# Four PSUM banks for the maxima's scores and one for the output, another order of blocks, and GpSimd for the parts of the turned maxima

## The chip, the cores and the metric

The program runs on one core of a Trainium2 chip. The metric is the device time of one execution in microseconds (us). The engines are TensorE (PE in the profile, its weight loads PEld), VectorE (DVE), ScalarE (ACT), GpSimd (POOL) and the queue from which DMAs are issued (SP). PSUM has eight banks of 128 x 512 fp32 elements; PE writes its products there.

## The reference, cut to what matters

One transformer layer on 4 sequences of 1024 tokens, 256 wide: a routed feed-forward part (8 experts, each token takes 2), an attention with 16 heads of 16, and the same feed-forward part again.

```python
x = x + 0.5 * ffn(layernorm(x))
x = x + attn(layernorm(x))        # adds its own residual and a second layernorm inside
x = x + 0.5 * ffn(layernorm(x))
# inside attn, for each of the 4 x 16 heads:
scores = (q @ k.T) * 0.25         # 1024 x 1024, causal
attn = softmax(scores)            # exp(score - row maximum) / row sum
out = attn @ v
```

Only the attention is touched by the change, and four lines of the transition into it.

## The kernel before, in words

The program has three parts in time: the first feed-forward part with the q, k and v projections, the attention, and the output projection with the second feed-forward part. The attention works on 16 groups (`NG`) of 4 heads of one sequence. Each engine runs its own list of instructions per group (`slot(g)`), in an order written out by hand, and waits on semaphores.

A group's work on PE is of three kinds.

- **Scores for the maxima** (`max_scores`, line 1404, 48 matmuls a group): queries x keys, in 38 units of 512 PSUM columns, each in a bank of `ms`. VectorE takes the negative row maximum of each unit (`max_read`; line 1431 for units with the causal diagonal, one instruction a head; line 1435 for whole ones). This runs one to two groups ahead. When all maxima of group g+1 stand, PE turns them (line 1397, the 39th entry), VectorE copies the turned tile out of PSUM (line 1413) and splits it with a cast, a subtraction, a cast and a subtraction (lines 1417 to 1423) into three bf16 parts, and SP places the parts by three DMAs as three more rows of the queries (`place_maxima`, line 1464; semaphore `mplaced`).
- **Scores for the exponentials** (`exp_unit`, line 1565, 48 matmuls a group): keys x queries with the maxima's rows, so that the maximum is already subtracted. The 12 blocks of a group (4 of the first half of the queries, 8 of the second) make 38 units in three banks `es`. The first unit of a group waits for `mplaced`. ScalarE takes the exponential of each unit into one of four buffers `probs` (line 1544). For blocks 0 to 3 and 8 to 11 GpSimd then zeroes what lies beyond the diagonal (line 1515).
- **Products** (`products`, line 1581): a block's probabilities by the values, fp32, 4 heads side by side in 32 columns of the array each; 8 records a block. They add up in a bank of `os`, one bank for each half of the queries. ScalarE copies each bank out when its half is complete (`copy_out`, line 1531, behind blocks 1 and 5 of its own order).

How these follow each other on PE is given by three tables with an entry a block: `MAXIMA` (how many entries of the maxima's stream go among that block's exponential units; `FIRST_MAXIMA` for group 0, `LAST_MAXIMA` for the last two groups), `MAXIMUM_FIRST` (whether such an entry comes first), and `PRODUCTS` (after which step, and for how many blocks, products are made; they run behind by at least two blocks). Blocks of products made at one place, or at the end of one block's steps and the start of the next, follow each other without scores between them. With the tables of before a group has products at nine places, three of them with two blocks.

Three banks serve the maxima's scores (`ms`), so PE may be two units ahead of VectorE:

```python
a.ms = ms = s.banks[3:6]
a.os = os_ = s.banks[6:8]
...
pe.wait_ge(mread, at(position - 2))
```

GpSimd's list for a group is the eight selects, and a copy of the next group's values behind block 2. SP's list for a group is: 12 loads of queries and keys for group g+2, 8 stores of group g-1, the three DMAs of `place_maxima(g+1)`, and 4 stores of inverted sums.

Of the kernel before, what the change touches and what calls it, by code (L numbers as in the profile page):

```python
# [18 lines left out]
ALU = mybir.AluOpType  # L19
ACT = mybir.ActivationFunctionType  # L20
# [32 lines left out]

FIRST = (39, 42, 47, 50)


CREDIT = 8

# [2 lines left out]

MAXIMA = (3, 3, 2, 3, 5, 4, 4, 3, 4, 3, 4, 1)
FIRST_MAXIMA = (6, 3, 2, 3, 5, 4, 4, 3, 4, 3, 4, 1)
LAST_MAXIMA = (3, 3, 2, 2, 3, 3, 3, 3, 2, 1, 0, 0)
MAXIMUM_FIRST = (1, 1, 1, 1, 0, 0, 1, 1, 1, 0, 0, 1)
BEHIND = -2
PRODUCTS = ((0, 0), (1, 2), (3, 1), (6, 1), (8, 2), (8, 1), (0, 0), (7, 2), (8, 1), (0, 0), (2, 1), (0, 1))


def at(events):
# [96 lines left out]
def ffn(nc, s, ctx, a, first):  # L169
# [96 lines left out]


    if first:
        ring, pb, pt, pr = [a.ms[2], a.es[2], *a.os], a.ms[1], a.es[0:2], a.ms[0]
    else:  # L270
        ring, pb, pt, pr = [*a.es, a.os[0]], a.os[1], a.ms[0:2], a.ms[2]
    pr_b = pr[:, 0:P // 2].bitcast(BF16)
    if first:

# [474 lines left out]
    def tensor(pe):  # L749
# [180 lines left out]
            pe.wait_ge(a.o_copied, at(2 * NG))  # L930
        slots(pe, slot)
        if first:
            pe.wait_ge(q.qk_rest, at(4 * (NCH - 1) + 1))
            a.first_scores(pe, FIRST[2], FIRST[3])
            pe.wait_ge(q.v_ready, at(2 * NCH))
            pe.wait_ge(q.qk_rest, at(4 * NCH))
# [303 lines left out]
def attention(nc, s, ctx):  # L1240
# [11 lines left out]
    early = 14  # L1252
    nkb = len(keys)
    half_blocks = CH // P
    assert nmax % 3 == 0
    offset = s.behind_v

    def sb(name, shape, dt=F32):
# [32 lines left out]
    below = sb("below", [P, CH], BF16)  # L1291
    masked_b = below[:, CH - P:CH]
    a.es = es = s.banks[0:3]
    a.ms = ms = s.banks[3:6]
    a.os = os_ = s.banks[6:8]

    consts, vones = sem("consts"), sem("vones")
    loaded = [sem(f"loaded{u}") for u in range(3)]
# [30 lines left out]

    def place(g, n):  # L1330

        return nmax + early + nmax * g.n + n, (early + n) % 3

    def placed(g):

# [55 lines left out]

    def max_scores(pe, entry, position, bank):
        g, n = entry
        pe.wait_ge(mread, at(position - 2))
        if n is None:
            pe.wait_ge(mfinal, at(g.n + 1))
            nc.tensor.transpose(ms[bank][0:GH * KT, 0:P], neg1[g.u][:].rearrange("p c i -> p (c i)"),  # L1397
                                s.ident[:]).then_inc(mscore, 1)
            return
        if n == 0:  # L1400
            pe.wait_ge(loaded[g.u], at(16 * 12 * (g.turn + 1)))
        i, lo, width, heads, diagonal = munits[n]
        for a, c in enumerate(heads):
            last = nc.tensor.matmul(ms[bank][:, a * width:(a + 1) * width], qs[g.u][0:ROWS, c, i * P:(i + 1) * P],  # L1404
                                    ks[g.u][0:ROWS, c, lo:lo + width], start=True, stop=True)
        last.then_inc(mscore, 1)

    def max_read(dve, entry, position, bank):
        g, n = entry
        dve.wait_ge(mscore, at(position + 1))  # L1410
        if n is None:
            t, r, m = turned, turned_rest, mparts[g.u]
            dve.tensor_copy(t[:], ms[bank][0:GH * KT, 0:P]).then_inc(mread, 1)
            dve.wait_ge(mread, at(position + 1))
            if not (isinstance(g.turn, int) and g.turn == 0):
                dve.wait_ge(mplaced[g.u], at(16 * 3 * g.turn))
            dve.tensor_copy(m[:, 0, :], t[:]).then_inc(mpart, 1)
            dve.wait_ge(mpart, at(5 * g.n + 1))
            dve.tensor_tensor(r[:], t[:], m[:, 0, :], ALU.subtract).then_inc(mpart, 1)
            dve.wait_ge(mpart, at(5 * g.n + 2))  # L1420
            dve.tensor_copy(m[:, 1, :], r[:]).then_inc(mpart, 1)
            dve.wait_ge(mpart, at(5 * g.n + 3))
            dve.tensor_tensor(m[:, 2, :], r[:], m[:, 1, :], ALU.subtract).then_inc(mpart, 2)
            return
        i, lo, width, heads, diagonal = munits[n]
        dst = neg1[g.u][:, heads[0]:heads[0] + len(heads), i:i + 1] if lo == 0 else \
            neg2[g.u][:, heads[0]:heads[0] + len(heads), i - CH // P:i - CH // P + 1]
        if diagonal:
            for a in range(len(heads)):
                part = ms[bank][:, a * width:(a + 1) * width]  # L1430
                last = dve.tensor_tensor_reduce(part, part, below[:, CH - width:CH], -1.0, 3.0e38, ALU.add, ALU.min,  # L1431
                                                dst[:, a, :])
            last.then_inc(mread, 1)
        else:
            dve.tensor_reduce(dst, ms[bank][:, 0:len(heads) * width].rearrange("p (h w) -> p h w", w=width), AX.X,  # L1435
                              ALU.max, negate=True).then_inc(mread, 1)
        if n == len(munits) - 1:
            dve.wait_ge(mread, at(position + 1))
            late = neg1[g.u][:, :, CH // P:KT]
            dve.tensor_tensor(late, late, neg2[g.u][:], ALU.min).then_inc(mfinal, 1)  # L1440

    def first_bank(position):

        if position < FIRST[0]:
            return 0
        return (position - FIRST[0]) % 2 if position < FIRST[2] else position % 3

    def first_scores(pe, lo, hi):

# [57 lines left out]
    def gpsimd(pool, lead):  # L1507
        def slot(g):
            for b, (j, half, start, width) in enumerate(keys):
                if b in sel_blocks:  # L1510
                    pool.wait_ge(expd, at(nexp * g.n + unit0[b + 1]))
                    pool.sem_inc(apart, 1)
                    part = probs[b % 4][:, :, 0:P]

                    pool.affine_select(out=part, in_=part, compare_op=ALU.is_ge, fill=0.0, base=0,  # L1515
                                       pattern=[[0, GH], [1, P]], channel_multiplier=-1).then_inc(kept, 1)
                if b == 2 and exists(g + 1):
                    pool.wait_ge(summed, at(nkb * g.n))
                    copy_values(pool, g + 1)
                lead_step(lead, g, b)  # L1520

        slots(slot)

    def scalar(act, lead):
        def copy_out(g, half):
            act.wait_ge(summed, at(nkb * g.n + (4 if half == 0 else nkb)))
            if exists(g + (-2)):
                old = g + (-2)
                act.wait_ge(stored[old.u], at(16 * GH * (old.turn + 1)))
                act.wait_ge(den_placed[old.u], at(16 * GH * (old.turn + 1)))  # L1530
            act.activation(oev[g.n % 2][:, half * CH:(half + 1) * CH], os_[half][:], ACT.Copy).then_inc(o_copied, 1)

        def slot(g):
            for b, (j, half, start, width) in enumerate(keys):
# [21 lines left out]
    def tensor(pe, lead):  # L1556
# [13 lines left out]
        def products(g, b):  # L1570
# [5 lines left out]
            if b == 0:  # L1576
                pe.wait_ge(v_copied, at(g.n + 1))
            if j == 0:
                pe.wait_ge(o_copied, at(2 * g.n - 1 + half))
            for c in range(GH):  # L1580
                last = nc.tensor.matmul(os_[half][SLOT * c:SLOT * (c + 1), start:CH], vs[g.n % 2][:, j, c, :],  # L1581
                                        probs[b % 4][:, c, 0:width], start=(j == 0),
                                        stop=(j == (half + 1) * CH // P - 1))
            last.then_inc(summed, 1)
# [81 lines left out]
```

## Time and the profile before

| | before |
|---|---|
| median of 3 runs | 1008.99 us (1007.57 to 1012.28) |
| the profiled execution, its own time | 1006.76 us |
| its span in the profile | 1005.0 us |
| the three parts in the span | about 0 to 335, 335 to 745, 745 to 1005 us |
| PE busy in the attention, 335 to 745 | 403.94 of 410 us |
| VectorE busy there | 388.97 us |
| ScalarE busy there | 305.94 us |
| GpSimd busy there | 96.83 us |

The profile is of one execution. Its own time lies 1.8 us above its span, and 2.2 us below the median of the runs. Busy time of PE is modelled, with matmuls overlapping, so it is read by the starts of the matmuls and not by their length. A semaphore's release is inferred.

### The profile page before, as it was taken

Reading aid. Unit: us, or ns where it says so; the run is one execution under the profiler, and the core shown is the slowest. Engines: PE = TensorE matmul, PEld = TensorE weight load, DVE = VectorE, ACT = ScalarE, POOL = GpSimd, SP = SyncE. Lnnn points to the kernel's source line nnn. Section 1 sums busy time; section 2 is a strip of 40 time slices with the busy share of each in tenths; the row PEclk is TensorE's granted clock in tenths of the full one; section 3 lists DMA queues with packets and bytes.
Section 4 is the critical chain, followed back from the end, with each engine's and each line's share of the span. In section 5 each row is a group of like instructions: output and inputs, shape, how many; then the busy total and the mean of one; then the engine's idle time right before and its main releaser. Section 6 shows DMA issues by size and latency. Waiting matters only on the chain.

```text
span 1005.0 us, 17657 instructions
## 1 busy us (share of the span) xinstructions
PE 956.5 (95%) x5602; PEld 569.3 (57%) x5602; DVE 831.5 (83%) x2445; ACT 511.8 (51%) x1053; POOL 264.9 (26%) x288
## 2 busy tenths in 40 slices
PE   6899998988998899999999999999998999999998
PEld 4678886766766433333333333333343777777776
DVE  6677777777677799999999999999868888888775
ACT  4235434414133577777777777777765333232310
POOL 1012204202021622121212212121443543435211
PEclk9999999999999999999999999999999999999999
DMA  6301121101032422222222223223320111110001
GB/s 214 98 1 64 57 70 64 58 6 63 1 95 65 139 77 66 67 71 68 70 67 71 77 77 77 76 76 77 69 84 12 44 64 64 63 49 16 19 22 42
DMA packets 55109, 64.32 MB, mean 64 GB/s; under 512 B 13824, under 2 KB 37360, under 8 KB 55024
## 3 DMA queue, kind: packets, MB, share of 16 engines
q1 hardware_dynamic: 54432, 62.47, 21.9%
q8 instruction: 43, 0.70, 0.3%
q10 hardware_dynamic: 592, 0.80, 0.2%
q14 instruction: 42, 0.34, 0.1%
HBM read 41.30 MB, written 21.23 MB: 62 GB/s over the span
## 4 chain that ended last, share of the span: by engine, by line
PE 65%; DVE 5%; ACT 2%; POOL 1%; issue 1%; DVEq 0%; ACTq 0%; POOLq 0%
PE bank L362 21%; PE bank L1581 14%; PE bank L1404 13%; PE bank L1565 13%; PE bank L836 2%; ACT b_probs L1544 1%; PE bank L354 1%; POOL b_ks L1377 1%; POOL a_part L496 1%; DVE c_acc L1049 1%; DVE c_st L317 1%; DVE bank L1431 0%; PE bank L785 0%; DVE c_eq L1010 0%; PE bank L1397 0%
## 5 line engine op out<-in xcount | busy, mean ns | idle before, releaser
L1544 ACT ACTIVATE b_probs<-bank 128x512 f32<-128x512 f32 (+1 forms) x608 | 302.4, 585 | 110.4 <-PE bank L1565 110.1
L1431 DVE CUSTOM_DVE_ANT_0 bank<-bank,b_below 128x384 f32<-128x384 f32 (+3 forms) x512 | 235.4, 516 | 11.1 <-PE bank L1404 9.7
L1404 PE MATMUL bank<-b_ks,b_qs 96*128 96x512 bf16 (+3 forms) x768 | 222.0, 330 | 16.4 <-DVE b_neg L1431 8.8
L1565 PE MATMUL bank<-b_qs,b_ks 99*128 99x512 bf16 (+3 forms) x768 | 214.5, 330 | 4.5 <-ACT b_probs L1544 4.3
L362 PE MATMUL bank<-we,a_xt 128*128 128x512 f32 x768 | 194.5, 405 | 0.9 <-DVE a_acc L1049 0.9
L362 PE MATMUL bank<-we,c_xt 128*128 128x512 f32 x768 | 186.2, 398 | 1.1 <-DVE c_acc L1049 0.9
L1515 POOL TENSOR_SCALAR_AFFINE_SELECT b_probs<-b_probs 128x512 f32<-128x512 f32 x128 | 84.3, 659 | 323.1 <-ACT b_probs L1544 320.0
L1435 DVE TENSOR_REDUCE b_neg<-bank 128x1 f32<-128x512 f32 x256 | 161.1, 680 | 2.6 <-PE bank L1404 1.2
L362 PEld LDWEIGHTS bank<-we,c_xt 128*128 128x128 f32 x768 | 142.3, 188 | 33.6 <-DVE c_acc L1049 2.0
L362 PEld LDWEIGHTS bank<-we,a_xt 128*128 128x128 f32 x768 | 142.7, 191 | 28.7 <-DVE a_acc L1049 1.4
L1581 PE MATMUL bank<-b_probs,b_vs 128*32 128x512 f32 (+3 forms) x1536 | 155.7, 500 | 1.2 <-POOL b_probs L1515 1.2
L1404 PEld LDWEIGHTS bank<-b_ks,b_qs 96*128 96x128 bf16 x768 | 67.3, 97 | 123.7 <-DVE b_neg L1431 54.9
L1565 PEld LDWEIGHTS bank<-b_qs,b_ks 99*128 99x128 bf16 x768 | 66.1, 98 | 107.8 <-ACT b_probs L1544 70.1
L1049 DVE SCALAR_TENSOR_TENSOR a_acc<-bank,a_mask,a_acc 128x256 f32<-128x256 f32 x192 | 81.7, 477 | 19.5 <-PE bank L362 18.8
L1049 DVE SCALAR_TENSOR_TENSOR c_acc<-bank,c_mask,c_acc 128x256 f32<-128x256 f32 x190 | 80.1, 477 | 19.8 <-PE bank L362 19.2
L490 POOL TENSOR_TENSOR xs<-a_acc,a_acc 128x256 f32<-128x256 f32 x32 | 25.2, 788 | 237.3 <-DVE a_acc L1049 237.3
L1431 DVE DVE_READ_ACCUMULATOR2_ANT b_neg<- 128x1 f32 x512 | 70.4, 137 | 0.0
L1581 PEld LDWEIGHTS bank<-b_probs,b_vs 128*32 128x32 f32 x1536 | 35.3, 109 | 57.1 <-ACT b_probs L1544 34.7
L490 POOL TENSOR_TENSOR xs<-c_acc,c_acc 128x256 f32 (+1 forms) x31 | 28.4, 916 | 94.1 <-DVE c_acc L1049 94.1
L362 PE MATMUL bank<-a_xt2r,a_wqk 128*128 128x512 f32 x192 | 46.4, 396 | 0.0
L333 ACT ACTIVATE c_std<-c_mv,eps 128x4 f32<-128x4 f32 x16 | 4.9, 303 | 80.4 <-DVE c_mv L322 80.4
L333 ACT ACTIVATE a_std<-a_mv,eps 128x4 f32<-128x4 f32 x16 | 4.8, 298 | 75.5 <-DVE a_mv L322 75.5
(136 smaller groups left out, 925.7 us busy)
## 6 DMA issues: line engine op xcount, KB each, us to landing
b_qs<-q_parts SPq DMA_DIRECT2D x96, 128.0 KB, 3.0
b_ks<-k_parts SPq DMA_DIRECT2D x96, 128.0 KB, 3.0
q_parts<-a_part SPq DMA_DIRECT2D x16, 384.0 KB, 2.6
k_parts<-a_part SPq DMA_DIRECT2D x16, 384.0 KB, 2.7
att_num<-b_oev SPq DMA_DIRECT2D x64, 64.0 KB, 2.2
c_num<-att_num SPq DMA_DIRECT2D x8, 512.0 KB
c_rec<-att_rec SPq DMA_DIRECT2D x16, 256.0 KB
out<-xs SPq DMA_DIRECT2D x7, 512.0 KB, 3.2
```

The lines of the kernel that those rows point to most:

```text
L317: last = dve.bn_stats(st_[:, t, :], src(t))
L362: last = nc.tensor.matmul(out_, wa if x_moves else xa_, xa_ if x_moves else wa, start=(n == 0), stop=(n == len(steps) - 1))
L490: pool.tensor_tensor(s.xs[:, row(c, t), :].rearrange("p a d -> p (a d)"), acc[t % 2][0][:], acc[t % 2][1][:], ALU.add).then_inc(q.x_ready, 1)
L836: last = nc.tensor.matmul(pt[pair][:, i * D:(i + 1) * D], att[par][:, h, t * P:(t + 1) * P], s.wp[:, h, :], start=(h == 0), stop=(h == DK ...
L1049: dve.scalar_tensor_tensor(out=dst[:], in0=ring[n][:, i * D:(i + 1) * D], scalar=mask[par][:, t, 2 * n + i:2 * n + i + 1], in1=base, op0=A ...
L1404: last = nc.tensor.matmul(ms[bank][:, a * width:(a + 1) * width], qs[g.u][0:ROWS, c, i * P:(i + 1) * P], ks[g.u][0:ROWS, c, lo:lo + width] ...
L1431: last = dve.tensor_tensor_reduce(part, part, below[:, CH - width:CH], -1.0, 3.0e38, ALU.add, ALU.min, dst[:, a, :])
L1435: dve.tensor_reduce(dst, ms[bank][:, 0:len(heads) * width].rearrange("p (h w) -> p h w", w=width), AX.X, ALU.max, negate=True).then_inc(mr ...
L1515: pool.affine_select(out=part, in_=part, compare_op=ALU.is_ge, fill=0.0, base=0, pattern=[[0, GH], [1, P]], channel_multiplier=-1).then_in ...
L1544: act.activation(probs[b % 4][:, heads[0]:heads[0] + hp, 0:width], es[exp_bank(g, unit)][:, 0:hp * width].rearrange("p (h w) -> p h w", w= ...
L1565: last = nc.tensor.matmul(es[exp_bank(g, unit)][:, a * width:(a + 1) * width], ks[g.u][:, c, j * P:(j + 1) * P], qs[g.u][:, c, first_q:fir ...
L1581: last = nc.tensor.matmul(os_[half][SLOT * c:SLOT * (c + 1), start:CH], vs[g.n % 2][:, j, c, :], probs[b % 4][:, c, 0:width], start=(j == ...
```

## The change

The maxima's scores get a fourth bank, and the output has one bank for both halves. PE may be three units ahead of VectorE. The product of a half's first block now waits until the other half has been copied out of the one bank. The tables get other values. VectorE only copies the turned maxima out of PSUM; the four instructions that make the parts are GpSimd's, behind its select of block 8 and ahead of that of block 9 (VectorE keeps them for group 0). In the transition from the first part, three scores wait for the third of four copies in place of the first, since the fourth bank is one that the first part uses.

```diff
+FIRST_SCORES = FIRST[2]
-MAXIMA = (3, 3, 2, 3, 5, 4, 4, 3, 4, 3, 4, 1)
-FIRST_MAXIMA = (6, 3, 2, 3, 5, 4, 4, 3, 4, 3, 4, 1)
+MAXIMA = (4, 4, 2, 0, 4, 5, 3, 6, 4, 4, 2, 1)
+FIRST_MAXIMA = (6, 5, 2, 0, 4, 5, 3, 6, 4, 4, 2, 1)
-MAXIMUM_FIRST = (1, 1, 1, 1, 0, 0, 1, 1, 1, 0, 0, 1)
+MAXIMUM_FIRST = (1, 0, 0, 0, 1, 1, 1, 1, 0, 0, 0, 1)
-PRODUCTS = ((0, 0), (1, 2), (3, 1), (6, 1), (8, 2), (8, 1), (0, 0), (7, 2), (8, 1), (0, 0), (2, 1), (0, 1))
+PRODUCTS = ((9, 1), (0, 1), (8, 0), (3, 1), (0, 1), (3, 2), (6, 1), (9, 2), (1, 0), (0, 1), (7, 2), (6, 0))
...
-            pe.wait_ge(q.qk_rest, at(4 * (NCH - 1) + 1))
+            pe.wait_ge(q.qk_rest, at(4 * (NCH - 1) + 3))
...
-    a.ms = ms = s.banks[3:6]
-    a.os = os_ = s.banks[6:8]
+    a.ms = ms = s.banks[3:7]
+    a.os = os_ = s.banks[7]
...
-        return nmax + early + nmax * g.n + n, (early + n) % 3
+        position = nmax + early + nmax * g.n + n
+        return position, position % 4
...
-        pe.wait_ge(mread, at(position - 2))
+        pe.wait_ge(mread, at(position - (2 if position < FIRST_SCORES + 4 else 3)))
...
+    def maxima_parts(engine, g, position):
+
+        t, r, m = turned, turned_rest, mparts[g.u]
+        engine.wait_ge(mread, at(position + 1))
+        if g.turn:
+            engine.wait_ge(mplaced[g.u], at(16 * 3 * g.turn))
+        engine.tensor_copy(m[:, 0, :], t[:]).then_inc(mpart, 1)
+        engine.wait_ge(mpart, at(5 * g.n + 1))
+        engine.tensor_tensor(r[:], t[:], m[:, 0, :], ALU.subtract).then_inc(mpart, 1)
+        engine.wait_ge(mpart, at(5 * g.n + 2))
+        engine.tensor_copy(m[:, 1, :], r[:]).then_inc(mpart, 1)
+        engine.wait_ge(mpart, at(5 * g.n + 3))
+        engine.tensor_tensor(m[:, 2, :], r[:], m[:, 1, :], ALU.subtract).then_inc(mpart, 2)
...
-            dve.tensor_copy(t[:], ms[bank][0:GH * KT, 0:P]).then_inc(mread, 1)
+            dve.wait_ge(mpart, at(5 * g.n))
+            dve.tensor_copy(turned[:], ms[bank][0:GH * KT, 0:P]).then_inc(mread, 1)
+            if g.n == 0:
+                maxima_parts(dve, g, position)
...
+                if b == 8 and exists(g + 1):
+                    pool.wait_ge(kept, at(len(sel_blocks) * g.n + sel_blocks.index(b) + 1))
+                    turn = [n for n, (entry, _, _) in enumerate(placed(g)) if entry[1] is None][0]
+                    maxima_parts(pool, g + 1, placed(g)[turn][1])
+                    pool.wait_ge(mpart, at(5 * (g.n + 1) + 5))
...
             if j == 0:
-                pe.wait_ge(o_copied, at(2 * g.n - 1 + half))
+                pe.wait_ge(o_copied, at(2 * g.n + half))
```

## Rows read from the trace of the kernel before

**Rows 1.** Chain that ended last, 300 to 760 us, shares by line.
```profile
by line: PE bank L1581 30.1%; PE bank L1565 28.0%; PE bank L1404 27.8%; PE bank L362 3.0%; PE bank L836 1.6%; ACT b_probs L1544 1.6%; POOL b_ks L1377 1.5%; DVE bank L1431 0.9%; POOL a_part L496 0.9%; issue 0.8%; PE bank L1397 0.7%; DVE a_xt
```

**Rows 2.** Engines' busy time in one group; columns PE, PEld, DVE, ACT, POOL, granted clock.
```profile
551.70:577.90 26.20, 26.17 (x194) 9.71 (x193) 25.74 (x88) 19.67 (x40) 5.61 (x9) 1.00 0.28 74
```

**Rows 3.** Timeline of PE through one group; start, length, instruction, records merged.
```profile
551.70 0.59 PE L1565 MATMUL bank<-b_qs,b_ks 99*128 99x512 bf16 x2
...
556.00 1.06 PE L1581 MATMUL bank<-b_probs,b_vs 128*32 128x512 f32 x8
557.00 0.39 PE L1565 MATMUL bank<-b_qs,b_ks 99*128 99x256 bf16 x2
...
566.01 0.38 PE L1565 MATMUL bank<-b_qs,b_ks 99*128 99x512 bf16 x1
566.36 0.40 PE L1404 MATMUL bank<-b_ks,b_qs 96*128 96x128 bf16 x4
...
567.25 0.38 PE L1565 MATMUL bank<-b_qs,b_ks 99*128 99x512 bf16 x1
567.66 0.39 PE L1404 MATMUL bank<-b_ks,b_qs 96*128 96x256 bf16 x2
567.89 0.38 PE L1565 MATMUL bank<-b_qs,b_ks 99*128 99x512 bf16 x1
568.20 1.92 PE L1581 MATMUL bank<-b_probs,b_vs 128*32 128x512 f32 x16
570.05 0.28 PE L1397 MATMUL bank<-ident,b_neg 128*32 128x128 f32 x1
...
571.33 0.38 PE L1565 MATMUL bank<-b_qs,b_ks 99*128 99x512 bf16 x1
...
577.94 0.60 PE L1565 MATMUL bank<-b_qs,b_ks 99*128 99x512 bf16 x2
```

**Rows 4.** Timeline of the other engines from the turned maxima to their placing.
```profile
570.38 0.28 DVE L1413 COPY b_turned<-bank 32x128 f32<-32x128 f32 x1
...
571.78 0.55 DVE L1431 CUSTOM_DVE_ANT_0 bank<-bank,b_below 128x384 f32<-128x384 f32 x1
571.88 1.81 SPq L1464 DMA_DIRECT2D b_qs<-b_mparts  x3
...
572.82 0.64 POOL L1515 TENSOR_SCALAR_AFFINE_SELECT b_probs<-b_probs 128x512 f32<-128x512 f32 x1 [12.85 <-ACT b_probs L1544]
```

**Rows 5.** Line 1464's DMAs from 500 to 600 us: issue to landing.
```profile
DMA to landing us min/median/max: 1.8/1.9/2.2
```

**Rows 6.** GpSimd's instructions by form, whole span; busy, mean ns, idle before.
```profile
L496 POOL TENSOR_TENSOR a_part<-a_rest,a_part 128x512 bf16<-128x512 f32 x32 | 36.6, 1166 | 24.3 <-ACT a_part L645 24.2
L490 POOL TENSOR_TENSOR xs<-a_acc,a_acc 128x256 f32<-128x256 f32 x32 | 25.2, 788 | 237.3 <-DVE a_acc L1049 237.3
...
L504 POOL TENSOR_TENSOR c_residb<-c_resid,bproj 128x1024 f32<-128x1024 f32 x8 | 19.3, 2407 | 16.2 <-ACT c_resid L339 16.2
...
L1377 POOL MEMSET b_ks<- 3x4096 bf16 x3 | 10.5, 3507 | 0.2
L1370 POOL COPY b_vs<-v_all 128x512 f32<-128x512 f32 x16 | 9.8, 612 | 0.1
...
L474 POOL TENSOR_SCALAR_AFFINE_SELECT ident<-ident 128x128 f32<-128x128 f32 x1 | 0.3, 294 | 0.2 <-POOL eps L472 0.2
...
L470 POOL MEMSET ident<- 128x128 f32 x1 | 0.2, 205 | 0.3 <-POOLq L1656 0.3
```

**Rows 7.** Timeline of GpSimd and VectorE near the end of the attention.
```profile
735.94 1.75 POOL L1515 TENSOR_SCALAR_AFFINE_SELECT b_probs<-b_probs 128x512 f32<-128x512 f32 x1 [0.34 <-ACT b_probs L1544]
735.98 1.21 DVE L1065 TENSOR_TENSOR c_att<-c_num,c_rec 128x1024 f32<-128x1024 f32 x1
```

**Rows 8.** PE's busy time and granted clock in two stretches next to each other.
```profile
723.80:727.20 3.40, 1.58 (x13) 1.00 0.69 123
727.25:730.60 3.35, 3.35 (x19) 0.50 0.56 187
```

More of the change, by code:

```diff
@@ L268, in ffn @@
     if first:
-        ring, pb, pt, pr = [a.ms[2], a.es[2], *a.os], a.ms[1], a.es[0:2], a.ms[0]
+        ring, pb, pt, pr = [a.ms[2], a.es[2], a.ms[3], a.os], a.ms[1], a.es[0:2], a.ms[0]
     else:
-        ring, pb, pt, pr = [*a.es, a.os[0]], a.os[1], a.ms[0:2], a.ms[2]
+        ring, pb, pt, pr = [*a.es, a.ms[3]], a.os, a.ms[0:2], a.ms[2]
     pr_b = pr[:, 0:P // 2].bitcast(BF16)
@@ L1254, in attention @@
     half_blocks = CH // P
-    assert nmax % 3 == 0
     offset = s.behind_v
@@ L1411, in max_read @@
         if n is None:
-            t, r, m = turned, turned_rest, mparts[g.u]
-            dve.tensor_copy(t[:], ms[bank][0:GH * KT, 0:P]).then_inc(mread, 1)
[L1414 to L1423, printed above, removed]
+            dve.wait_ge(mpart, at(5 * g.n))
+            dve.tensor_copy(turned[:], ms[bank][0:GH * KT, 0:P]).then_inc(mread, 1)
+            if g.n == 0:
+                maxima_parts(dve, g, position)
             return
@@ L1445, in first_bank @@
             return 0
-        return (position - FIRST[0]) % 2 if position < FIRST[2] else position % 3
+        return (position - FIRST[0]) % 2 if position < FIRST[2] else position % 4
     def first_scores(pe, lo, hi):
@@ L1530, in copy_out @@
                 act.wait_ge(den_placed[old.u], at(16 * GH * (old.turn + 1)))
-            act.activation(oev[g.n % 2][:, half * CH:(half + 1) * CH], os_[half][:], ACT.Copy).then_inc(o_copied, 1)
+            act.activation(oev[g.n % 2][:, half * CH:(half + 1) * CH], os_[:], ACT.Copy).then_inc(o_copied, 1)
         def slot(g):
@@ L1578, in products @@
             if j == 0:
-                pe.wait_ge(o_copied, at(2 * g.n - 1 + half))
+                pe.wait_ge(o_copied, at(2 * g.n + half))
             for c in range(GH):
-                last = nc.tensor.matmul(os_[half][SLOT * c:SLOT * (c + 1), start:CH], vs[g.n % 2][:, j, c, :],
+                last = nc.tensor.matmul(os_[SLOT * c:SLOT * (c + 1), start:CH], vs[g.n % 2][:, j, c, :],
                                         probs[b % 4][:, c, 0:width], start=(j == 0),
```

## The prediction

> **What bounds the kernel now.** I read the chain of waits first, for 300 to 760 us, since the change touches only the attention. The reader is to see three PE lines with 86% of it (products 30.1%, exponential scores 28.0%, maxima's scores 27.8%) and no other engine above 2% [rows 1]. Next I read busy time in one group: of 26.2 us PE is busy 26.17, VectorE 25.74, ScalarE 19.67, GpSimd 5.61, at full clock [rows 2]. Two engines are nearly full, so taking work from one alone buys little. Third, PE's timeline. A group lasts from its first exponential score at 551.70 to the next group's at 577.94, 26.24 us [rows 3]; all groups from 1 to 13 do so. I split it by the starts of matmuls.
>
> A 512-column unit normally takes 0.22 us from start to start. Two stretches are longer because the bank still has to be read by VectorE: 566.01 to 566.36 (0.13 too much) and 567.25 to 567.66 (0.19) [rows 3]. Three shorter waits add about 0.10; together 0.43, with 0.05 for weights that then load late.
>
> Products at one place cost more than their columns. One block of 512 takes 1.00 us (556.00 to 557.00), two take 1.85 (568.20 to 570.05), so the first carries 0.15 that the second doesn't; and they start 0.31 after the last score (567.89 to 568.20), 0.09 over the normal step [rows 3]. Each place costs 0.24 us, nine a group 2.1.
>
> **The change part by part.**
>
> *Order.* I wrote out the new tables. The twelve product blocks stand at seven places: 10 and 11 of the group before, 0 and 1, 2 and 3, 4, 5 and 6, 7, then 8 and 9. The first two pairs span the end of one block's steps and the start of the next. Two places less: -0.47 us a group.
>
> By the Trainium skill ("TensorEngine Tiling (Array Packing)", section "Key Properties") a change of tiling mode drains TensorE. It gives no price; the row does.
>
> *Fourth bank and VectorE's relief.* VectorE's own path around the turn lasts from 570.38 to 571.78, 1.40 us [rows 4]; the copy with its step is 0.31 of this, so 1.09 leaves. Its 25.74 become 24.65. I walked PE, VectorE and ScalarE through the new order with the durations of before and a bank wait four units back: no wait for VectorE is left. The same walk with the old order gives 26.26 us a group against 26.24 measured, with the two long waits in their places. So PE's own time a group is 26.24 - 0.43 - 0.05 - 0.47 = 25.29.
>
> *One output bank.* The product of block 4 needs the first half copied out. In the walk ScalarE ends this copy 12.36 us into the group and PE comes to block 4 at 12.59; for block 0 the distance is the same. Cost nothing, with 0.2 us of cover. If ScalarE is later than that, each 0.1 us costs a group 0.1 and the kernel 1.5.
>
> *Parts on GpSimd.* This is where I expect the gain to go. Before, VectorE had finished the parts at 571.85, SP issued at 571.88 for 1.81 us [rows 4], and the last of three DMAs, issued at 573.1, landed 1.9 later [rows 5], at 575.0: 2.9 us ahead of the first exponential score that waits for it. Now GpSimd starts behind its select of block 8. Step by step, from a group's first exponential score:
>
> - Last score of block 8: 571.33 - 551.70 = 19.63 before [rows 3]. Less one place of products (0.24) and the bank waits ahead of it (0.35, with 0.05 for late weights): 19.0.
> - Its exponential and the select end at 573.46, 2.13 behind that score's start [rows 3, 4]: 21.13. A wait of GpSimd on its own semaphore: three memsets have 0.2 us idle ahead of them, 0.06 each [rows 6]: 21.2.
> - The four instructions on 32x128. Their price isn't in the trace. Partitions don't matter to GpSimd's rows (3x4096 takes 0.86 ns an element of a partition, 128x128 205 ns), so 128 elements count. Subtractions: 256 elements take 788 ns, 1024 take 2407 [rows 6], a line of 2.1 ns an element that gives 0.52 at 128; the form with bf16, 512 in 1166, lies lower and gives 0.42 with a start of 0.19; I take 0.45. Casts: 512 elements copied take 612, a select of 128 takes 294 [rows 6]; I take 0.28. With three waits of 0.06: 2 x 0.45 + 2 x 0.28 + 0.18 = 1.64: 22.84. Bounds: four times the memset's 0.205 and the waits, 1.0; twice 0.788, twice 0.612 and three waits of 0.2 (the select of 128 waited that), 3.4. The wider rows are two and four times this work, so I stay near the lower third.
> - SP, three issues and the landing: 3.14 as before (571.85 to 575.0): 25.98. PE's wait ends 0.07 later: 26.05.
>
> PE comes there at 25.29 and waits 0.76 us. So the chain through GpSimd sets the group's length: 26.05 in place of 26.24, -0.19. Behind the waiting score on PE stand all scores and products of the next group; VectorE runs dry for about 0.4 us of it, ScalarE for all of it.
>
> By the Trainium skill ("GPSIMD Engine Reference", section "4.1 Engine selection") elementwise work belongs on VectorE, since GpSimd takes twice as long with two inputs. Twice VectorE's 0.28 for the subtractions, with 0.28 for the casts, makes 1.86 and a group of 26.27, no gain at all; the rows above put it at 1.64.
>
> *Selects behind the parts.* Block 9's select now waits for the parts, until 22.9. Its exponentials end near there and its products come at 24 or later: nothing. SP's four inverse stores and the next group's loads go out some 2 us later; the loads are for scores that PE makes in the group's second half.
>
> *Transition.* Three scores wait for the third copy in place of the first; VectorE reads them only behind the fourth, as before: nothing. Group 0 gains what the others do. *Last group:* no maxima stand between its products and one bank serves both halves; the walk has 0.5 us more.
>
> **Sum.** Thirteen groups at -0.19 are -2.5, group 0 -0.2, the last +0.5: -2.2 us. The span 1005.0 becomes 1002.8, the execution 1006.8 becomes 1004.6. The runs' median lies 2.2 above the profiled execution, so 1006.8 us. Each 0.1 us of the four instructions moves it by 1.5.
>
> **Rivals.**
>
> *GpSimd is quick.* At 1.2 us or less for the chain of four, a group takes 25.6 or less; with group 0 and the last that is -0.63 x 13 - 0.6 + 0.5 = -8.3, 1000.7; at the lower bound of 1.0, -11, 998. For it: a memset of 128 elements takes 0.205. Against: it reads nothing, and the select of 128 takes 0.294. So 998 to 1004.
>
> *GpSimd is slow, the other side.* The place is the same first exponential score. From 1.83 us on a group is longer than before, from 2.15 on the kernel is slower by over 0.5%. What would do it: waits of 0.2 in place of 0.06 (+0.4), or GpSimd held up by VectorE, as at 735.94, where a select takes 1.75 us in place of 0.64 beside a VectorE instruction of two SBUF inputs that starts with it [rows 7]. At 2.4 us: +0.57 x 13 + 0.6 + 0.5 = +8.5, 1017.5. Against: the selects keep their 0.64 beside line 1431 all through the attention, and that is what VectorE runs there.
>
> By the Trainium skill ("SBUF — State Buffer", section "Who interferes with whom") a VectorE instruction with two SBUF inputs blocks a GpSimd one that reads SBUF; line 1431 has one and a PSUM bank. The trace agrees.
>
> *The output bank is late.* ScalarE misses the cover of 0.2 us; at 0.5 us late in each half, once of it ahead of block 8: +0.3 to +0.6 a group on top of the forecast, 1011 to 1016. Against: ScalarE is idle a quarter of the time.
>
> *The clock.* After a stretch of 3.4 us with PE busy only 1.58, the granted clock is 0.50 for the next 3.4 us [rows 8]. A wait of 0.8 leaves PE far busier; only with the slow case of 2.5 us or more might it join.
>
> **Chances.** Within 0.5% (5 us; about what a measurement of this kernel can tell from no change): the forecast 0.44 and a mild form of the bank's lateness 0.04, 0.48. Faster by more: 0.32, for a quick GpSimd. Slower by more: 0.20, slow GpSimd 0.14, output bank 0.06. The range takes four instructions of 1.1 to 2.15 us: 1009.0 - 9.7 to 1009.0 + 5, 999 to 1014. The forecast's own range is 1004 to 1010.
>
> **What the profile would show.** Products at seven places a group, each pair 1.85 us or less. No wait of line 1404 for VectorE of over 0.1 us. VectorE 24.7 us busy a group. Lines of `maxima_parts` on GpSimd: 1.6 us from first start to last end, starting 21.2 us into the group. PE idle 0.6 to 0.9 us ahead of each group's first line 1565 with SP's placing as its releaser; no such wait means the parts were quicker than 0.9 us. Groups of 26.05 us. Wrong it would be if the casts or subtractions take other times than 0.28 and 0.45, if a wait on GpSimd's own semaphore costs 0.2, or if the landing takes longer than 1.9.

## The result, and the profile after

The changed kernel takes 1018.52 us (median of 14 runs, 1013.95 to 1025.58), the kernel before in the same session 1010.27 (14 runs, 1007.37 to 1013.24). The ratio is 1.0089, 95% interval 1.0061 to 1.0116: slower by 0.9%, where the forecast said 1006.8 and "within 0.5%". The profiled execution took 1022.13, its span is 1020.4 (before: 1006.76 and 1005.0). In the experiments below one run, of experiment 2, took 1669.94 us at a granted clock of 0.725; it is left out of that ratio, and nothing here explains it.

The page of the changed kernel: busy times of PE and VectorE, the chain that ended last, and the row of the exponential scores.

```profile
PE 955.2 (94%) x5602; PEld 585.4 (57%) x5602; DVE 819.0 (80%) x2385; ACT 513.1 (50%) x1053; POOL 284.3 (28%) x348
...
PE 55%; POOL 4%; ACT 4%; DVE 4%; DMA 3%; issue 2%; SPq 2%; POOLq 0%; DVEq 0%; ACTq 0%
...
L1578 PE MATMUL bank<-b_qs,b_ks 99*128 99x512 bf16 (+3 forms) x768 | 223.8, 333 | 18.2 <-DMA b_qs<-b_mparts 13.8
```

PE is as busy as before. The chain now runs through GpSimd, SP and a DMA, and the scores of line 1578 have 13.8 us of idle time ahead of them that the placing of the maxima's parts ends. PE's own waits, 374 to 709 us (us in total, times, longest):

```profile
PE bank L1578 <- DMA b_qs<-b_mparts: 13.2, 13, 2.3
```

It is the only wait in that list; before, PE had none there. The first scores of the thirteen groups 1 to 13 have 13.2 us of it, 1.0 each, and the longest is 2.3. Two kinds of group hide in this sum.

**A group as forecast.** One group's busy times, in the columns of [rows 2]:

```profile
510.45:536.54 26.09, 25.50 (x193) 10.54 (x193) 24.93 (x84) 19.71 (x40) 6.95 (x13) 1.00 0.28 74
```

Its end, from the timeline of all engines, in the columns of [rows 4]:

```profile
530.98 0.64 POOL L1523 TENSOR_SCALAR_AFFINE_SELECT b_probs<-b_probs 128x512 f32<-128x512 f32 x1 [12.67 <-ACT b_probs L1557]
...
531.68 0.28 POOL L1416 CAST b_mparts<-b_turned 32x128 bf16<-32x128 f32 x1
...
532.04 0.42 POOL L1418 TENSOR_TENSOR b_turned_rest<-b_turned,b_mparts 32x128 f32<-32x128 f32 x1
...
532.52 0.28 POOL L1420 CAST b_mparts<-b_turned_rest 32x128 bf16<-32x128 f32 x1
...
532.95 0.42 POOL L1422 TENSOR_TENSOR b_mparts<-b_turned_rest,b_mparts 32x128 bf16<-32x128 f32 x1 [0.15 <-POOL b_mparts L1420]
...
533.40 1.81 SPq L1472 DMA_DIRECT2D b_qs<-b_mparts  x3
...
536.55 0.39 PE L1578 MATMUL bank<-b_qs,b_ks 99*128 99x512 bf16 x1 [0.59 <-DMA b_qs<-b_mparts]
```

The parts start 21.23 us into the group and take 1.69; the next group's first exponential score comes 3.18 after their end. The group lasts 26.09 us; undisturbed ones have 26.07 to 26.10. The forecast said 21.2, 1.64, 3.21 and 26.05.

**A group that is not.** Group 9, from 588.7, lasts 27.57. PE at its end:

```profile
613.82 0.38 PE L1406 MATMUL bank<-b_ks,b_qs 96*128 96x512 bf16 x1
616.27 0.39 PE L1578 MATMUL bank<-b_qs,b_ks 99*128 99x512 bf16 x1 [2.06 <-DMA b_qs<-b_mparts]
```

From start to start that is 2.45 us, where an undisturbed group has 0.95. GpSimd was in time; the third of the placing's DMAs, issued at 613.11, took 3.1 us in place of 1.9. What the DMA engines moved, in four windows: a whole stretch (613.5 to 615.5), its 0.05 us from 613.75, then 614.6 to 614.9 and 614.9 to 615.2.

```profile
q1 hardware_dynamic: 96, 0.02, 4.6%
q8 instruction: 1, 0.02, 3.8%
issues: line engine op xcount, KB each, median us to landing
att_rec<-b_rcp SPq DMA_DIRECT2D x2, 4.0 KB, 2.0
b_qs<-b_mparts SPq DMA_DIRECT2D x1, 8.0 KB, 3.1
...
q8 instruction: 1, 0.02, 150.0%
...
DMA packets 0, 0.00 MB, mean 0 GB/s; under 512 B 0, under 2 KB 0, under 8 KB 0
...
DMA packets 6, 0.00 MB, mean 3 GB/s; under 512 B 6, under 2 KB 6, under 8 KB 6
```

In 613.75 to 613.80 a packet of the instruction queue q8 starts; 3.8% of sixteen engines' 2 us are 1.2 us, so it holds one engine until about 614.97. Of the small packets up to 615.2 all have gone by 614.6 but six, and these come just after 614.9. The trace names no DMA engine for a packet, but this fits one engine's share of the small packets standing behind one packet of instructions.

By the Trainium skill ("DMA: Bandwidth & Descriptors", section "Queues, rings and completion order") a DMA engine goes round its queues by whole packets, and finishes one before it turns to the next. The trace agrees as far as it goes: no small packet from 614.6 to 614.9, and six as soon as the packet of 1.2 us is over.

**And the clock.** The same kernel around the late landing of group 3's placing (columns of [rows 2]; the granted clock is the third figure from the end):

```profile
428.00:430.60 2.60, 0.33 (x4) 0.00 (x0) 1.21 (x2) 0.60 (x1) 0.63 (x1) 1.00 0.07 13
...
431.45:434.80 3.35, 3.35 (x23) 1.03 (x21) 2.09 (x10) 1.90 (x4) 0.64 (x1) 0.50 0.48 141
```

PE had 0.33 us of work in 2.6 us; 0.75 us after it went on, the granted clock stood at 0.50 (1.2 GHz) for 3.4 us, and the next group took 27.65 in place of 26.08. This came after three of the four late landings, and nowhere else in groups 1 to 13.

**Where the 15.4 us of the two profiled executions lie**, by the starts of the groups' first exponential scores: 3.5 ahead of group 0, where two stretches at half clock (from 202.7 and 288.1 us) fall before any changed instruction; group 0 +2.1; groups 1 to 13 +8.3 (the order and relief -2.1, late landings +4.2, clock after them +6.2); group 14 +0.5; the rest +1.0. The first item is taken for chance: it is absent in the next profile, and the runs of before scatter by as much. The cause of the last is not known.

### The profile page after: what moved, and what is told of

It is laid out like the page before. It is cut to its first block, busy times and chain, and to the rows that moved or that the text cites. A ratio compares the mean times of both kernels' runs of the same rounds, so it can differ in the third digit from the quotient of the medians.

```text
span 1020.4 us, 17675 instructions
## 1 busy us (share of the span) xinstructions
PE 955.2 (94%) x5602; PEld 585.4 (57%) x5602; DVE 819.0 (80%) x2385; ACT 513.1 (50%) x1053; POOL 284.3 (28%) x348
## 3 DMA queue, kind: packets, MB, share of 16 engines
HBM read 41.30 MB, written 21.23 MB: 61 GB/s over the span
## 4 chain that ended last, share of the span: by engine, by line
PE 55%; POOL 4%; ACT 4%; DVE 4%; DMA 3%; issue 2%; SPq 2%; POOLq 0%; DVEq 0%; ACTq 0%
PE bank L364 23%; PE bank L1578 10%; PE bank L1594 10%; PE bank L1406 9%; ACT b_probs L1557 3%; DMA b_qs<-b_mparts 3%; PE bank L838 2%; SPq L1472 2%; PE bank L356 1%; POOL b_probs L1523 1%; POOL b_ks L1379 1%; POOL b_mparts L1422 1%; POOL b_turned_rest L1418 1%; POOL a_part L498 1%; POOL b_mparts L1416 1%
## 5 line engine op out<-in xcount | busy, mean ns | idle before, releaser
L1406 PE MATMUL bank<-b_ks,b_qs 96*128 96x512 bf16 (+3 forms) x768 | 224.9, 334 | 17.2 <-DVE b_neg L1439 7.2
L1578 PE MATMUL bank<-b_qs,b_ks 99*128 99x512 bf16 (+3 forms) x768 | 223.8, 333 | 18.2 <-DMA b_qs<-b_mparts 13.8
L364 PE MATMUL bank<-we,a_xt 128*128 128x512 f32 x768 | 197.8, 410 | 1.1 <-DVE a_acc L1051 1.1
L1443 DVE TENSOR_REDUCE b_neg<-bank 128x1 f32<-128x512 f32 x256 | 164.0, 683 | 14.4 <-PE bank L1406 12.9
L364 PEld LDWEIGHTS bank<-we,c_xt 128*128 128x128 f32 x768 | 143.4, 190 | 33.5 <-DVE c_acc L1051 1.4
L1594 PE MATMUL bank<-b_probs,b_vs 128*32 128x512 f32 (+3 forms) x1536 | 150.0, 500 | 3.5 <-POOL b_probs L1523 3.3
L1578 PEld LDWEIGHTS bank<-b_qs,b_ks 99*128 99x128 bf16 x768 | 71.9, 98 | 119.2 <-ACT b_probs L1557 52.7
L1406 PEld LDWEIGHTS bank<-b_ks,b_qs 96*128 96x128 bf16 x768 | 71.7, 99 | 90.7 <-DVE b_neg L1443 27.2
L1594 PEld LDWEIGHTS bank<-b_probs,b_vs 128*32 128x32 f32 x1536 | 37.7, 110 | 77.7 <-ACT b_probs L1557 43.4
L498 POOL TENSOR_TENSOR a_part<-a_rest,a_part 128x512 bf16<-128x512 f32 x32 | 36.6, 1164 | 24.4 <-ACT a_part L647 24.3
```

Of the source, the lines that this page charges most:

```text
L364: last = nc.tensor.matmul(out_, wa if x_moves else xa_, xa_ if x_moves else wa, start=(n == 0), stop=(n == len(steps) - 1))
L498: pool.tensor_tensor(part[j][:, 2, :], rest[j % 2][:], part[j][:, 1, :], ALU.subtract).then_inc(q.qk_lo, 1)
L1578: last = nc.tensor.matmul(es[exp_bank(g, unit)][:, a * width:(a + 1) * width], ks[g.u][:, c, j * P:(j + 1) * P], qs[g.u][:, c, first_q:fir ...
L1594: last = nc.tensor.matmul(os_[SLOT * c:SLOT * (c + 1), start:CH], vs[g.n % 2][:, j, c, :], probs[b % 4][:, c, 0:width], start=(j == 0), st ...
```

## The experiments

**1. The changed kernel again**, no edit.

> The changed kernel itself, for a second profile. In the first one 10 of 14 groups waited 0.73 us for the placing of the maxima and lasted 26.08 us; in the other four the third DMA landed 0.9 to 1.7 us late, each time beside a 16 KB packet of the instruction queue, and three of these four were followed by a stretch of half clock. Theory A (fetches of PE's instructions fall at fixed places of the program and delay the landing): the same groups, or nearly, are late again, with such a packet beside each. Theory B (late landings are chance): other groups, or another number of them, with no packet beside some. Both expect 26.08 us for the undisturbed groups.

Measured: 1017.73 us, span 1016.0. The front is as before (group 0 starts at 339.47, before 339.69). Groups 1 to 13 take 26.08 to 26.10, but for 27.21, 27.49 and 27.65 (late landings) and twice 27.7 (half clock from 423.4 and 662.3). The placings for groups 1, 3, 10 and 12 are late again, 3.0 to 3.6 us from issue to landing. The same four groups in two executions: the lateness is no chance.

**2. The parts ahead of block 8's select.**

```diff
             for b, (j, half, start, width) in enumerate(keys):
+                if b == 8 and exists(g + 1):
+                    turn = [n for n, (entry, _, _) in enumerate(placed(g)) if entry[1] is None][0]
+                    maxima_parts(pool, g + 1, placed(g)[turn][1])
+                    pool.wait_ge(mpart, at(5 * (g.n + 1) + 5))
                 if b in sel_blocks:
...
-                if b == 8 and exists(g + 1):
-                    pool.wait_ge(kept, at(len(sel_blocks) * g.n + sel_blocks.index(b) + 1))
...
```

> The four instructions of the parts stand ahead of GpSimd's select of block 8 in place of behind it; nothing else differs from the changed kernel. Theory A (the chain over GpSimd, the placing and PE's first score of a group sets the group's length, and what makes it slow is that this wait is open): the parts start 18.7 us into a group in place of 21.2, the placing lands at 23.6 to 25, PE doesn't wait, a group takes 25.3 us, no landing and no clock stretch shows, and the kernel takes about 998 us, 1.2% under before. Theory B (one output bank or the new order costs the time, GpSimd is beside it): groups stay at 26.1 and the kernel near 1018.

Measured: 1002.55 us (median of all 9 runs), ratio 0.9926 [0.9901, 0.9952]. All groups 1 to 13 take 25.31, PE waits for no placing, and there is no half clock among them. This number bears out PE's own 25.29, the sum of the order, the bank waits' end and an output bank that costs nothing; it does not measure these one by one. The third DMA now lands 1.9 us ahead of its reader (1.7 once), but no packet of q8 starts in the 1.9 us after its issue, so a late landing was not put to the test. The last group grew to 37.1: the parts now wait for the turned maxima with the selects behind them, and 10.2 us of the group are at half clock.

**3. The parts on VectorE**, the order and the banks as changed.

```diff
-            if g.n == 0:
-                maxima_parts(dve, g, position)
+            maxima_parts(dve, g, position)
...
-                if b == 8 and exists(g + 1):
-                    pool.wait_ge(kept, at(len(sel_blocks) * g.n + sel_blocks.index(b) + 1))
...
```

> The changed kernel with the parts made by VectorE in all groups, as before the change; four score banks, one output bank and the new order stay. Theory A: the placing lands over 2 us ahead of its use, no open landing; VectorE's 25.74 us of work set the group, about 25.9 to 26.0; the kernel takes 1006 to 1008 us, at or just under before (1010). Theory B (output bank or order are at fault): slower than before, 1015 or more, with PE waiting at its products.

Measured: 1007.0 us (10 runs), ratio 0.9967 [0.9947, 0.9987]; groups of 26.00, group 14 at 30.9, one landing of 2.3 us that nothing waited for. The order and the banks alone are worth a little; moving the parts costs the changed kernel 11 us.

**4. One more cast on GpSimd.**

```diff
         engine.wait_ge(mread, at(position + 1))
+        if g.n > 0:
+            engine.tensor_copy(m[:, 0, :], t[:]).then_inc(again, 1)
+            engine.wait_ge(again, at(g.n))
```

> The changed kernel with the first cast on GpSimd made twice, with a wait between (0.28 + 0.08 us by the changed kernel's profile). Theory A: each undisturbed group grows by 0.36 us to 26.44, the kernel by 14 x 0.36 = 5 us or a little more against the changed one, to 1023 to 1026, some 1.5% over before; the wait ahead of a group's first exponential score grows from 0.73 to 1.09. Theory B (GpSimd off the path): no growth.

Measured: 1026.79 us (4 runs), ratio 1.0175 [1.0134, 1.0216]; undisturbed groups 26.43, +0.35 for a cast of 0.28 and its step of 0.08. So GpSimd's chain sets the group. A miss in detail: PE's gap ahead of the first exponential score stayed 0.95. The 0.35 is spent earlier: block 9's select comes later and PE's products wait for it. Groups 1, 3, 10 and 12 are late a third time.

**5. Each part placed as soon as it is made.**

```diff
-        sp.wait_ge(mpart, at(5 * g.n + 5))
-        for part in range(3):
+        for part, made in enumerate((1, 3, 5)):
+            sp.wait_ge(mpart, at(5 * g.n + made))
```

> The changed kernel with one thing other: SP issues the DMA of each part as soon as that part is made, in place of all three behind the last. GpSimd's four instructions stay where they are, behind the select of block 8. Theory A (the open landing is what costs): the last DMA lands 1.24 us earlier, 0.5 us ahead of its use; undisturbed groups take 25.3 us; where a fetch of PE's instructions falls on the landing (1.5 us late) a wait of up to 1 us is left; group 14 stays slow. About 1001 to 1005 us. Theory B (GpSimd's instructions in this place hold up something else, such as the select of block 9): 26.1 us a group as in the changed kernel.

Measured: 997.86 us (4 runs), ratio 0.9891 [0.9858, 0.9924], better than expected. In the columns of [rows 2]:

```profile
518.70:544.03 25.33, 25.33 (x196) 10.58 (x194) 24.73 (x83) 19.60 (x40) 6.94 (x13) 1.00 0.27 75
```

Only one issue and landing now stands behind the last part: it lands 0.5 us ahead of the score that needs it (543.86 and 544.37), for which PE waits 0.73 us in the changed kernel. Two lines on SP take the whole loss of groups 1 to 13 away; group 14 takes 33.5. There is luck in it: in groups 1, 3, 10 and 12 a packet of q8 starts 1.8 to 2.1 us after the third DMA's issue, just too late to hold it up (that for group 3 took 2.3 and landed 0.1 ahead of its reader). A landing of 2.6 to 3.6 would have outlasted this cover; the wait of up to 1 us that was expected for it did not occur in this profile, and is not refuted.

**6. Parts first, and those of the first and the last group on VectorE.**

```diff
-            if g.n == 0:
+            if g.n in (0, NG - 1):
                 maxima_parts(dve, g, position)
...
+                if b == 8 and exists(g + 2):
...
                 if b in sel_blocks:
```

> Parts ahead of the select of block 8 as in e1_parts_first, and for the last group (made within group 14) by VectorE as before the change. In e1 GpSimd sat 6.3 us in group 14 waiting for the turned maxima, with the selects of blocks 8 to 10 behind it and PE behind these, and group 14 took 37.05 us against 31.35 before. Theory A: groups 1 to 13 at 25.31 as in e1, group 14 near 30.9 as in e2_parts_vector, the kernel 5 us or more under e1, 994 to 998 us, 1.3 to 1.5% under before. Rival: group 14 is slow in e1 for the clock or the new order; then it stays near 35 and the kernel near 1002.

Measured: 995.47 us (6 runs, 994.15 to 998.83), ratio 0.9864 [0.9838, 0.989]: the fastest version, 1.4% under before. Groups of 25.31, group 14 at 31.1. The third DMA lands 1.9 us ahead of its reader (1.7 once); the longest landing in these profiles exceeds the usual one by 1.8. As in experiment 2, no late one came to test it.

```profile
518.69:544.00 25.31, 25.31 (x194) 10.64 (x193) 24.73 (x84) 19.60 (x41) 6.99 (x13) 1.00 0.29 76
```

**7. Only the parts moved**: the kernel before, with GpSimd's `maxima_parts` and nothing else of the change.

> The kernel before with one part of the change alone: GpSimd makes the parts, behind its select of block 8; three score banks, two output banks and the old order stay. Theory A (worked out by the walk of the old order with the measured 1.69 us for the four instructions): parts start at 21.8 us into a group, the last placing lands at 26.6, a group takes 26.7 us, with four or so late landings open as well: 1020 to 1026 us, 1 to 1.5% slower than before. Theory B: no change, since GpSimd is idle four fifths of the time.

Measured: 1018.58 us (5 runs), ratio 1.0076 [1.0049, 1.0103], just under what was expected. One group, in the columns of [rows 2]:

```profile
535.65:562.30 26.65, 26.31 (x194) 9.63 (x195) 25.26 (x84) 19.79 (x41) 6.98 (x13) 1.00 0.26 72
```

So an undisturbed group takes 26.65. The placings for groups 1, 3 and 10 are late by 1.0 to 1.5 us, yet here no half clock follows. Around the longest one, PE's work and clock:

```profile
426.74:428.93 2.19, 0.38 (x4) 0.04 (x1) 1.31 (x3) 0.60 (x1) 0.63 (x1) 1.00 0.08 15
429.00:432.40 3.40, 3.40 (x32) 1.55 (x33) 2.49 (x11) 2.69 (x6) 0.64 (x1) 1.00 0.39 107
```

**8. Only the order**: the kernel before, with the four tables of the change.

> The kernel before with one part of the change alone: the four tables, with three score banks, two output banks and the parts on VectorE. Theory A (the order needs the fourth bank, since it puts the maxima's scores closer together): PE waits for VectorE's reads at many places, by the walk 28.1 us a group, about +26 us, 1035 us. Theory B (the order alone brings the two saved places of products): 25.8 us a group, 1004 us.

Measured: 1037.85 us (2 runs), ratio 1.0273 [1.0231, 1.0316]. One group, and then the waits of 370 to 737 us:

```profile
540.10:568.28 28.18, 27.16 (x195) 10.01 (x194) 26.01 (x88) 19.98 (x41) 5.58 (x9) 1.00 0.27 69
```

```profile
PEld bank L1404 <- DVE b_neg L1435: 52.1, 144, 0.6
PEld bank L1404 <- DVE b_neg L1431: 44.1, 91, 1.1
...
DVE b_neg L1435 <- PE bank L1404: 21.3, 39, 0.8
```

The maxima's scores wait for VectorE and VectorE for the scores: with three banks the new order doesn't work; with four it does (experiment 3). So the parts of the change don't add up: order alone +1.9 us a group, parts alone +0.4, all together -0.16. Four score banks alone and the single output bank alone were not run.

**9 and 10. The instruction stream moved.** 24 and 64 instructions of PE more at the very beginning, which repeat the turn of the router's weights.

```diff
-                    for h in range(DK):
+                    for h in [h for _ in range(7) for h in range(DK)]:    # 17 in the second
                         last = nc.tensor.transpose(...)
```

> The changed kernel with six more turns of the router's weights at its very beginning, which puts 12 weight loads and 12 matmuls (24 instructions of PE) ahead of all else. They redo a transpose that is done anyway, so that all values stay. In the two profiles of the changed kernel each 16 KB packet of the instruction queue q8 starts at the same PE instruction (the 3527th in group 1 both times), some 256 of PE's instructions after the one before. Theory A (the late third DMA is late because such a packet is under way beside it): PE issues some 15 of these instructions per us, so 24 more move every such packet 1.6 us to the front of the placing. In groups 1, 3, 10 and 12 it started 0.95 to 2.2 us after the second DMA's issue; now it starts 0.3 us after it or before, too early for the third, and no other group's packet gets into that stretch (the nearest, 5.1 to 6.6 us behind, come to 3.5 to 5). So none of the 13 groups 1 to 13 has a last landing over 2.5 us, each takes 26.1 us, and with 1 us for the added work the time is 1009 to 1014, ratio to before 1.000 to 1.005. Theory B (the lateness belongs to what those groups do: their loads and stores on the queue, or their number): the same four groups are late by 1 to 1.7 us, and the time is 1016 to 1022.

Measured: 1014.18 us (10 runs), ratio 1.0054 [1.0027, 1.0082]. The landings for groups 1, 8 and 10 are late (3.3, 2.8 and 3.2 us); those for 3 and 12 are not. Neither forecast holds: the late groups changed, against theory B, but not to none. Counted from the attention's first exponential score, the packets beside the placings for groups 1 and 10 came at the same PE instruction as before (the changed kernel's two profiles agree within nine), those near the placings for 3, 8 and 12 some 50 to 70 instructions sooner, where a rigid shift would be 24. So the packets don't move rigidly by the number of instructions added.

> The same with sixteen more turns, 64 instructions of PE. Theory A: the packets of q8 move 4.2 us to the front; those that started 5.1 to 6.6 us after the second DMA's issue (groups 4, 6, 8 and 13) now start 0.9 to 2.4 us after it, and these four groups are late by 0.9 to 1.7 us each; groups 1, 3, 10 and 12 take 26.1 us. The time is 1013 to 1022, as that of the changed kernel. Theory B: groups 1, 3, 10 and 12 are late again, and 4, 6, 8 and 13 are not.

Measured: 1019.74 us (one run). The landings for groups 4, 6, 8 and 13 take 3.4, 3.5, 2.6 and 3.4 us, and those for 1, 3, 10 and 12 take 1.9: the four groups that theory A named, and no other. Here the packets beside these four came 59 to 71 instructions sooner than in the changed kernel, for a shift of 64. The placing for group 6 (500 to 504 us: DMA queues; then PE's timeline):

```profile
q8 instruction: 1, 0.02, 2.1%
...
b_qs<-b_mparts SPq DMA_DIRECT2D x1, 8.0 KB, 3.5
```
```profile
500.88 0.38 PE L1406 MATMUL bank<-b_ks,b_qs 96*128 96x512 bf16 x1
503.48 0.39 PE L1578 MATMUL bank<-b_qs,b_ks 99*128 99x512 bf16 x1 [2.22 <-DMA b_qs<-b_mparts]
```

Nothing in the attention differs from the changed kernel but where PE's instructions lie in their stream. A forecast of the late groups by name from the packets' places came true, so the packets are the cause of the late landings; experiment 9 shows that the places themselves can't always be forecast.

**11. Only the last group's parts on VectorE.**

```diff
-            if g.n == 0:
+            if g.n in (0, NG - 1):
                 maxima_parts(dve, g, position)
...
-                if b == 8 and exists(g + 1):
+                if b == 8 and exists(g + 2):
```

> The changed kernel, with the parts of the last group alone (made in group 14) on VectorE. If the parts on GpSimd are what lengthens group 14 over the 31.35 us of before (31.84 and 34.88 in the two profiles of the changed kernel, with products waiting for selects that stand behind the parts), it takes 30.5 to 31.3 us here, and the time is 1014 to 1017, 1 to 3 below the changed kernel's 1018.5. If it is the new order of the blocks, or a clock that falls there for another reason, group 14 stays at 31.8 or more. Groups 1 to 13 stay as they are in the changed kernel, late ones 1, 3, 10 and 12.

Measured: 1014.79 us (10 runs), ratio 1.0042 [1.001, 1.0074], 3.7 under the changed kernel's median. The two ratios' intervals overlap, so the profile has to decide. Groups 1 to 13 are as in the changed kernel, with late landings for 1, 3, 10 and 12. Group 14 takes 29.44; the windows show it here, in the changed kernel and before (the granted clock is the third figure from the end):

```profile
722.99:752.43 29.44, 27.23 (x190) 11.13 (x191) 20.13 (x55) 23.46 (x48) 12.09 (x12) 1.00 0.33 84
```
```profile
723.07:754.91 31.84, 27.31 (x189) 11.13 (x190) 18.78 (x51) 23.46 (x48) 13.18 (x16) 1.00 0.33 80
```
```profile
709.16:740.51 31.35, 29.13 (x190) 10.90 (x189) 21.04 (x56) 24.04 (x49) 12.09 (x12) 0.95 0.30 78
```

The 31.35 of before held a stretch at half clock [rows 8], worth some 1.6 us. So at full clock the parts on GpSimd lengthen this group by 2.4, most of which the clock of before hid in the first comparison. The chain of the changed kernel through it (start, length, what):

```profile
745.33 0.32 ACT b_probs L1557
745.65 1.13 issue
746.78 1.16 POOL b_mparts L1416
...
748.92 0.43 POOL b_mparts L1422
...
749.55 0.63 POOL b_probs L1523
750.18 0.14 issue
750.32 0.85 PE bank L1594 x8
```

The turned maxima come late in this group, so the parts go ahead of two selects that PE's products need. VectorE's rows beside them:

```profile
743.82 1.22 DVE L1067 TENSOR_TENSOR c_att<-c_num,c_rec 128x1024 f32<-128x1024 f32 x1
746.58 1.20 DVE L1067 TENSOR_TENSOR c_att<-c_num,c_rec 128x1024 f32<-128x1024 f32 x1
```

The cast that takes 0.28 elsewhere takes 1.16 here, and ends 0.16 behind line 1067.

By the Trainium skill ("SBUF — State Buffer", section "Who interferes with whom") such a VectorE instruction, with both inputs in SBUF, contends with a GpSimd instruction that reads SBUF, and the one that starts first has the ports they share to itself until it ends. The trace agrees: the VectorE instruction started 0.20 ahead of the cast, which took 1.16 us against 0.28 without one beside it.

**All late landings of the third DMA** (over 2.5 us) in the seven profiles (of six kernels) in which PE waits for the placing. The half-clock stretches are those of groups 1 to 13 and begin between 0.7 us ahead of the waiting score's start and 1.5 behind it.

| kernel | late for groups | us to landing | half clock from |
|---|---|---|---|
| changed, first | 1, 3, 10, 12 | 3.4, 3.6, 3.1, 2.8 | 373.4, 431.4, 670.4 |
| changed, again | 1, 3, 10, 12 | 3.6, 3.0, 3.0, 3.5 | 423.4, 662.3 |
| one more cast | 1, 3, 10, 12 | 3.5, 2.9, 3.0, 3.4 | 373.1 |
| last on VectorE | 1, 3, 10, 12 | 3.5, 3.3, 2.8, 3.1 | 373.4, 431.4, 670.3 |
| 24 more | 1, 8, 10 | 3.3, 2.8, 3.2 | 607.5 |
| 64 more | 4, 6, 8, 13 | 3.4, 3.5, 2.6, 3.4 | 503.8, 691.6 |
| parts alone | 1, 3, 10 | 2.9, 3.4, 3.0 | none |

A 16 KB packet of q8 is under way beside each of the 26, and starts 0.0 to 1.6 us after the third DMA's issue. In the same profiles no such packet goes with a landing of 2.5 us or less. Half clock comes with 12 of them.

## Why the prediction was wrong

**Right, with its sizes.** PE's own time a group: 25.29 forecast, 25.31 measured once nothing waits (experiments 2 and 6). Bank waits gone: PE has none. VectorE: 24.65 forecast, 24.9 measured. Output bank: PE never waits for it. The transition: none seen. The parts' start 21.2, casts 0.28 (both), subtractions 0.42 for 0.45, which is 1.5 times VectorE's 0.28 and not twice. The three steps between them were too low: 0.08, 0.06 and 0.15, 0.30 in sum for 0.18. The chain of four came to 1.69 for 1.64, in part because the two errors have opposite signs. The group at 26.08 for 26.05, PE's wait at 0.73 for 0.76. The first two rivals, which turned on GpSimd's speed and held 0.46 of the chance, were about a term that was right to 0.05 us. That the slow rival named 1017.5, near the measured 1018.5, is a coincidence: it needed a chain of 2.4 us, and outside group 14 no chain was held up.

**The step that failed** is "SP, three issues and the landing: 3.14 as before". In undisturbed groups it is 3.13. But before, the landing lay 2.9 us ahead of its reader, and one of 3.6 us would have cost nothing; the change used this cover up and made every landing count. The constant then had to be the distribution of the landing, and in four of GpSimd's 15 placings it is 0.9 to 1.8 us longer. [rows 5] already shows a maximum of 2.2 beside the median of 1.9, and the text named a longer landing as a way to be wrong, but gave it no chance and no price.

**The clock rival was priced wrongly.** It was dismissed with "a wait of 0.8 leaves PE far busier". The waits that the late landings make are 1.9 to 2.7 us from start to start in the changed kernel, and half clock follows eight of the twelve in three profiles (the first, experiment 1, and experiment 11, which runs the same code up to group 14), at 1.6 us for 3.4 us of it (the stretches from 373.4 last 6.8 and cost 3.1).

**Group 14** was not in the sum. "Block 9's select waits: nothing" holds in the 13 groups before, with little to spare (experiment 4), and fails here, where the turned maxima come late: +2.4.

**The sum again**, with what was measured: 13 groups at -0.16 and group 0, -2.3; four late landings, +5.9 (PE's gap over its undisturbed 0.95: 1.77, 1.14, 1.42 and 1.57 in the second profile); two stretches at half clock, +3.2; group 14, +2.4; together +9.2, against +8.3 between the medians. Left out are the half clock within group 14, which each side has in some runs (one stretch in the profile of before, none and two in those of the changed kernel), and 0.9 us behind the attention in both profiles, whose cause is not known. The number of stretches varies from run to run, and with it the time: the changed kernel's runs at a granted clock of 0.987 to 0.988 take 1014 to 1017, those at 0.977 to 0.978 take 1025 to 1026.

**Open.** Why a packet of q8 comes at one PE instruction rather than another (experiment 9), and why half clock follows 12 late landings and not the other 14: the waits with it are 1.9 to 2.7 us, those without 1.7 to 2.7, so their length alone does not decide it. Nor was it pursued why group 14 has one such stretch before and none to two in the other profiles.

## What to carry to other kernels

A latency that is moved from under cover into the open is not priced at its median: every rare long case, and what the engine's clock does after the long wait, now counts. Where a chain ends in several small transfers, issue each as its input is ready; here that gave back 20 us for two changed lines, though with 0.5 us of cover it still rests on where the rare cases fall; putting the whole chain earlier (experiment 6) gave 1.9 us of cover, about what the longest landing seen here needs. Moving the work to another engine without either made the kernel 0.8% slower. And an engine that takes over work does so in every group: look at the group where that work is late, and at what is queued behind it.

## What the runs showed of the hardware

- A small DMA (8 KB in 256-byte packets) that normally lands 1.9 us after its issue takes 2.6 to 3.6 when a 16 KB packet of the instruction queue q8 starts 0.0 to 1.6 us after its issue (26 of 26 in the table). With a packet that started 0.4 us ahead of the issue (before, group 5) or 1.8 and 2.1 behind it (experiment 5) it took 1.9 to 2.3. These packets go with PE's instruction stream: 43 in the span for 11204 matmuls and weight loads. Adding 64 instructions at the kernel's beginning changed which groups of a loop that starts over 300 us later are slow.
- GpSimd on 32x128: casts 0.28 us, two-input subtractions 0.42, and 0.06 to 0.15 from the end of one to the start of the next that waits for it.
- A GpSimd cast beside a VectorE instruction with two SBUF inputs took 1.16 us in place of 0.28, and 1.22 in experiment 2.
